# First offset convolution of each deformable layer in two row parts, column transposes between them, first batch of offsets loaded before the first column windows

## The chip, the cores and the metric

The kernel runs on one core of a Trainium2 chip. The time is the device time of one execution in microseconds; the number compared is the median over several executions. Engines of the core: PE (matmul, with PEld for its weight loads), DVE (vector), ACT (scalar), POOL (here only memsets and DMA issue), SP (DMA issue).

## What is computed

The input is 8 images of 16 channels, 64 x 64, float32. Four blocks follow each other: a gated scan over rows and columns; an inverted bottleneck (hidden convolution, depthwise 3 x 3, projection); two deformable convolutions; and two distance convolutions with batch norm. The change touches the two deformable convolutions. Each computes offsets by a plain 3 x 3 convolution, samples the image at the shifted places for the 9 taps, and contracts the samples with the weights:

```python
def deform_conv(x, w, b, ow, ob):
    off = conv2d(x, ow, ob).reshape(Bn, K, 2, Hh, Ww) * OFFSET_SCALE
    cy = iy[None, None, :, None] + dy[None, :, None, None] + off[:, :, 0]
    cx = ix[None, None, None, :] + dx[None, :, None, None] + off[:, :, 1]
    ...
    samp = gather(y0i, x0i, (1 - wy) * (1 - wx)) + gather(y0i, x0i + 1, (1 - wy) * wx) + ...
    out = jnp.einsum('bckhw,ock->bohw', samp, w.reshape(w.shape[0], Cin, K))
h = jax.nn.relu(group_norm1(deform_conv(x, w1, b1, ow1, ob1), g1, be1)) + x
h = jax.nn.relu(group_norm1(deform_conv(h, w2, b2, ow2, ob2), g2, be2)) + h
```

## The kernel before

The program of each engine is written out by hand, with semaphores between the engines; every engine runs its own list in the order written. Both deformable layers (L = 0 and 1) run the same code. The image lies in SBUF at `XA`, 128 partitions (8 images x 16 channels), rows padded. A layer has an opening stage and a sampling stage.

**Opening stage.** The offset convolution is cut into four blocks of 16 rows, m = 0 to 3. `convolve(m)` (L1301) uses the PE array as 16 tiles of 32 x 32: for each of the 9 taps, 4 groups of partitions i (two images each), 2 axes and 2 halves h of the block (8 rows of 64, so 512 columns), one matmul, in all 144. Results stand in four PSUM banks, 4 to 7 for even m and 0 to 3 for odd m (`conv_bank`). float32 matmuls show as two pairs of weight load and matmul in the trace, so 288 pairs a block. ACT copies the four banks with the bias into `RAW` (`copy_offsets`, L1075, by the line of its operation L1082); DVE bounds them and adds a ramp (`bound_offsets`, L714; L720 and L722) and takes the largest value (`reach`, L725, L727). SP stores the block to the DRAM tensor `offsets` in four transfers of 256 KB (`store_offsets`, L450, L455), then rearranges it there into `offsets_by_batch`, a batch being 4 rows of output with all taps (`arrange_batch`, L460; the issues carry L472; 10 transfers for batch 0 and 6 for each next one). Batch 0 needs rows 0 to 4 of the offsets. POOL loads a batch into SBUF, spread over partitions, four transfers of 576 or 624 KB (`load_batch`, L1520, L1528).

Between `convolve(0)` and `convolve(1)` PE transposes the image into columns (`turn_columns`, L1316, 64 matmuls that show as 128 pairs, L1320), ACT and DVE copy the results (L1072, L711), POOL stores them to the DRAM tensor `columns` (`store_columns`, L1493, L1501) and loads windows of them back by chunks (`load_windows`, L1506, L1515). DVE spreads the windows (L422).

The order of PE's opening stage:

```python
convolve(0)
...
    turn_columns(g_)
...
convolve(1)
...
convolve(2)
pe.wait_ge(s_cve, 16 * L + 8)
convolve(3)
pe.wait_ge(s_cve, 16 * (L + 1))
```

**Sampling stage.** 16 batches of 3 units. For each batch ACT computes distances (`distances`, L1085, L1089) as soon as it is loaded, DVE clips them (L739), and for each unit ACT makes two y terms (`y_terms`, L1091, L1098 and L1099), DVE three products (L745 to L747), PE the sample matmuls (L1341, L1346), ACT copies the samples (L1109), and every second batch PE contracts them (L1364). On ACT, `distances(L, 0)` and the y terms of units 0 and 1 stand behind `copy_offsets(L, 2)`, those of unit 2 behind `copy_offsets(L, 3)`. On DVE, `bound_offsets(L, 3)` stands behind batch 0. The first sample matmul waits for all copies of convolution 3.

## Time and profile before

| what | us |
|---|---|
| median of 3 runs | 822.86 (821.83 to 826.68) |
| the profiled execution's own time | 825.47 |
| its span, first to last instruction | 823.7 |
| opening stage, first layer (first matmul of convolution 0 to last of convolution 3) | 223.84 to 282.86 |
| opening stage, second layer | 476.12 to 531.35 |
| mean granted TensorE clock | 0.923 of full speed |

Times in a timeline are microseconds from the start of the span; a row of a timeline merges instructions of one line that follow closely, with their count (an x count is one of trace records, so of pairs for PE), and in brackets the idle time of the engine before it and what ended it. "Issue" there means that the profile shows nothing that the engine waited for. A few matmul records can be missing or fall into a neighbouring row, so counts can be off by some per cent. A stretch's row gives busy time and record count of each engine, the granted clock, the DMA share (mean busy share of the 16 DMA engines) and GB/s.

### The profile page before, as it was taken

Reading aid. Unit: us, or ns where it says so; the run is one execution under the profiler, and the core shown is the slowest. Engines: PE = TensorE matmul, PEld = TensorE weight load, DVE = VectorE, ACT = ScalarE, POOL = GpSimd, SP = SyncE. Lnnn points to the kernel's source line nnn. Section 1 sums busy time; section 2 is a strip of 40 time slices with the busy share of each in tenths; the row PEclk is TensorE's granted clock in tenths of the full one; section 3 lists DMA queues with packets and bytes.
Section 4 is the critical chain, followed back from the end, with each engine's and each line's share of the span. In section 5 each row is a group of like instructions: output and inputs, shape, how many; then the busy total and the mean of one; then the engine's idle time right before and its main releaser. Section 6 shows DMA issues by size and latency. Waiting matters only on the chain.

```text
span 823.7 us, 30308 instructions
## 1 busy us (share of the span) xinstructions
PE 638.3 (77%) x13948; PEld 426.9 (52%) x13948; DVE 588.9 (71%) x839; ACT 461.3 (56%) x624; POOL 136.3 (17%) x229
## 2 busy tenths in 40 slices
PE   3449999999997767888887588658878788749482
PEld 1224545467874346565555465347555555527251
DVE  6994350211342899999999744699999999984456
ACT  2725252532321668888888341557888889441513
POOL 1000000000023232333320004423333330000000
PEclk9869999999999779999999889869999999959596
DMA  4000000000037967777772006988777773000002
GB/s 170 0 0 3 3 2 3 2 18 4 12 91 230 371 206 257 257 244 250 247 237 101 2 11 190 347 277 266 243 244 251 258 242 127 3 1 4 1 3 103
DMA packets 28778, 108.73 MB, mean 132 GB/s; under 512 B 10612, under 2 KB 15412, under 8 KB 24552
## 3 DMA queue, kind: packets, MB, share of 16 engines
q0 software_dynamic: 14400, 86.80, 31.6%
q1 hardware_dynamic: 14248, 19.97, 7.8%
q8 instruction: 110, 1.80, 0.9%
q14 instruction: 20, 0.16, 0.1%
HBM read 91.84 MB, written 19.65 MB: 135 GB/s over the span
## 4 chain that ended last, share of the span: by engine, by line
PE 50%; DVE 37%; issue 6%; ACT 6%; DMA 1%; SPq 0%; DVEq 0%; ACTq 0%
PE psum L1261 14%; PE psum L1308 10%; DVE arena L746 7%; DVE arena L747 7%; DVE arena L745 6%; PE psum L1341 6%; PE psum L1237 5%; PE psum L1364 5%; PE psum L1453 4%; DVE arena L422 4%; DVE arena L739 3%; PE psum L1320 2%; PE psum L1460 2%; PE psum L1274 2%; DVE arena L622 1%
## 5 line engine op out<-in xcount | busy, mean ns | idle before, releaser
L1341 PE MATMUL psum<-arena 64*64 64x297 f32 (+4 forms) x4512 | 225.3, 348 | 77.4 <-DVE arena L747 72.4
L1341 PEld LDWEIGHTS psum<-arena 64*64 64x64 f32 x4512 | 162.9, 137 | 140.0 <-DVE arena L747 83.2
L1109 ACT ACTIVATE arena<-psum 128x792 f32<-128x792 f32 (+1 forms) x96 | 84.7, 883 | 65.1 <-PE psum L1341 58.4
L1528 POOL DMA_DIRECT2D arena<-offsets_by_batch x128 | 80.0, 639 | 224.2 <-DVE arena L747 163.7
L1261 PE MATMUL psum<-arena 32*32 32x512 f32 x3456 | 115.1, 597 | 0.3 <-DVE arena L669 0.3
L1308 PE MATMUL psum<-arena 32*32 32x512 f32 x2304 | 86.6, 646 | 19.3 <-issue 13.5
L745 DVE SCALAR_TENSOR_TENSOR arena<-arena 128x792 f32<-128x792 f32 (+3 forms) x96 | 92.6, 965 | 5.7 <-ACT arena L1099 4.3
L1261 PEld LDWEIGHTS psum<-arena 32*32 32x32 f32 x3456 | 73.6, 103 | 39.9 <-issue 13.8
L747 DVE SCALAR_TENSOR_TENSOR arena<-arena 128x792 f32<-128x792 f32 (+3 forms) x96 | 92.3, 961 | 0.0
L746 DVE SCALAR_TENSOR_TENSOR arena<-arena 128x792 f32<-128x792 f32 (+3 forms) x96 | 92.2, 961 | 0.0
L1099 ACT ACTIVATE arena<-arena 128x792 f32<-128x792 f32 (+3 forms) x96 | 88.2, 918 | 0.0
L1098 ACT ACTIVATE arena<-arena 128x792 f32<-128x792 f32 (+3 forms) x96 | 87.8, 915 | 0.0
L1045 ACT ACTIVATE arena<-psum,arena 128x512 f32<-128x512 f32 x48 | 29.8, 686 | 92.1 <-PE psum L1261 92.1
L1089 ACT ACTIVATE arena<-arena 128x2304 f32<-128x2304 f32 (+1 forms) x32 | 72.7, 2272 | 11.3 <-DMA arena<-offsets_by_batch 11.3
L1308 PEld LDWEIGHTS psum<-arena 32*32 32x32 f32 x2304 | 49.6, 106 | 52.4 <-issue 39.0
L659 DVE TENSOR_SCALAR arena<-arena 128x2048 f32<-128x2048 f32 x12 | 14.7, 1231 | 84.8 <-ACT arena L1045 84.8
L1364 PE MATMUL psum<-arena 64*64 64x256 f32 x1152 | 68.1, 381 | 2.3 <-ACT arena L1113 2.3
L1237 PE MATMUL psum<-arena 128*128 128x512 f32 x96 | 45.4, 621 | 21.7 <-DVE arena L630 21.7
L1501 POOL DMA_DIRECT2D columns<-arena x16 | 9.9, 760 | 302.7 <-DVE arena L711 237.3
L1082 ACT ACTIVATE arena<-psum,arena 128x512 f32<-128x512 f32 x32 | 19.7, 687 | 61.1 <-PE psum L1308 61.1
L1453 PE MATMUL psum<-arena 32*32 32x512 f32 x1152 | 44.1, 663 | 12.3 <-DVE arena L906 10.8
L1364 PEld LDWEIGHTS psum<-arena 64*64 64x64 f32 x1152 | 43.4, 131 | 18.2 <-ACT arena L1113 2.5
(148 smaller groups left out, 683.1 us busy)
## 6 DMA issues: line engine op xcount, KB each, us to landing
arena<-offsets_by_batch POOLq DMA_DIRECT2D x112, 576.0 KB, 7.9
arena<-offsets_by_batch POOLq DMA_DIRECT2D x16, 624.0 KB, 7.6
offsets<-arena SPq DMA_DIRECT2D x32, 256.0 KB, 9.0
offsets_by_batch<-offsets SPq DMA_DIRECT2D x184, 24.0 KB
arena<-columns POOLq DMA_DIRECT2D x24, 160.0 KB, 9.5
columns<-arena POOLq DMA_DIRECT2D x8, 320.0 KB, 6.7
arena<-in_x SPq DMA_DIRECT2D x4, 512.0 KB, 5.2
out<-arena SPq DMA_DIRECT2D x8, 256.0 KB, 2.2
```

What stands on the lines that cost most here:

```text
L745: v.scalar_tensor_tensor(term(0), term(0), 0.0, part(tx), ALU.min, ALU.mult)
L746: v.scalar_tensor_tensor(term(1), term(1), 1.0, part(tx), ALU.subtract, ALU.mult)
L747: v.scalar_tensor_tensor(term(2), part(ty), 0.0, part(tx), ALU.min, ALU.mult).then_inc(s_g, 1)
L1098: a.activation(term(0), part, ACT.Copy, scale=-1.0)
L1099: a.activation(term(1), part, ACT.Abs).then_inc(s_nd, 1)
L1109: ins = a.activation(ap(SAMP + n // 2 % 2 * SPAR + n % 2 * SLOTS * K * SX + u * WB[0], [[SR, 2], [SX, KR], [1, w]]), ap_ps(bank, [[CH, 2], ...
L1237: t_.matmul(ps(ch % 4, 0, CH), cols(W_HID + t * P, P), cols(XIN + ch * CH, CH), start=True, stop=True).then_inc(s_c1, 1)
L1261: ins = t_.matmul(ps_q(j, dw_bank(t, half) + i), cols(W_DIAG + (t * K + k) * Q, Q, Q * i, Q), ap(T_PAD[t % 4] + row * PW + k % 3, [[PW, CR ...
L1308: ins = t_.matmul(ps_q(2 * axis + h, conv_bank(m) + i), cols(W_CONV[L] + (axis * K + t) * Q, Q, Q * i, Q), ap(XA + (BLK * m + 8 * h + t // ...
L1341: ins = t_.matmul(ps_t(s, bank + r, first * K * w, many * K * w), window, ap(g_at(unit, d0) + first * TW + s * w, [[GS + TW, many], [SLOTS ...
L1364: ins = t_.matmul(ps_t(r, bank, (2 - k // 3) * SX, GR * SX), weights_, ap(SAMP + j % 2 * SPAR + r * SR + k * SX, [[K * SX, GR], [1, SX]], ...
L1528: g.dma_start(cols(in_at(n, 0), 2 * in_rows(n) * W, 64 * r + 32 * half, 32), bass.AP(batch_d.tensor, 2 * (4 * r * NB + n) * INS, [[0, QW / ...
```

## The change

Convolution 0 is cut by rows: of each 8-row half of the block first rows 0 to 4 (`FIRST = 5`, 320 columns a matmul, banks 4 to 7), and after the transposes rows 5 to 7 (192 columns, banks 0 to 3). The banks of convolutions 1, 2 and 3 swap accordingly. ACT's copies and DVE's bounding of block 0 are cut in the same way, the second pieces behind the column copies; `written` and `stored` give the new semaphore counts. SP stores rows 0 to 4 of the first half (two transfers) and rearranges batch 0 before it stores the rest of the block (four transfers). POOL issues the load of batch 0 ahead of the first window load and that of batch 1 ahead of the second. ACT no longer waits for the whole image before its first copies.

```diff
+FIRST = 5
...
-        def ps_q(quadrant, bank):
-
-            return psum[quadrant * Q:(quadrant + 1) * Q, bank, 0:CH]
+        def ps_q(quadrant, bank, off=0, n=CH):
+
+            return psum[quadrant * Q:(quadrant + 1) * Q, bank, off:off + n]
...
-        def conv_bank(m):
-
-            return 4 if m % 2 == 0 else 0
+        def conv_bank(m, first=0):
+
+
+            return 0 if m % 2 == 0 and m + first > 0 else 4
...
+        def written(L, m, end=CR):
+
+
+            return 20 * L + 4 * m + (8 if m or end == CR else 4)
+
+        def stored(L, m):
+
+
+            return (64 if m else 96) * (L + 1)
...
             def store_offsets(L, m):
-                sp.wait_ge(s_d1, 4 * L + m + 1)
+                sp.wait_ge(s_d1, 5 * L + m + 2)
+                for h in range(2):
+                    store_rows(m, h, FIRST if m == h == 0 else 0, CR)
+
+            def store_rows(m, h, first, end):
+
                 for axis in range(2):
-                    for h in range(2):
-                        sp.dma_start(bass.AP(off_d.tensor, axis * B * KP * N + (2 * m + h) * CH,
-                                             [[N, 2 * KP], [2 * KP * N, 4], [1, CH]]),
-                                     ap(D1 + m % 2 * NATS, [[CH, 4], [1, CH]], 64 * axis + Q * h, Q)
-                                     ).then_inc(s_ds[m], 16)
+                    sp.dma_start(bass.AP(off_d.tensor, axis * B * KP * N + (2 * m + h) * CH + first * W,
+                                         [[N, 2 * KP], [2 * KP * N, 4], [1, (end - first) * W]]),
+                                 ap(D1 + m % 2 * NATS + first * W, [[CH, 4], [1, (end - first) * W]],
+                                    64 * axis + Q * h, Q)).then_inc(s_ds[m], 16)
...
-                sp.wait_ge(s_ds[min(SLOTS * n + SLOTS, H - 1) // BLK], 64 * (L + 1))
+                m = min(SLOTS * n + SLOTS, H - 1) // BLK
+                sp.wait_ge(s_ds[m], stored(L, m) if n else 96 * L + 32)
...
             for L in range(2):
+                sp.wait_ge(s_d1, 5 * L + 1)
+                store_rows(0, 0, 0, FIRST)
+                arrange_batch(L, 0)
                 store_offsets(L, 0)
-                arrange_batch(L, 0)
                 arrange_batch(L, 1)
                 arrange_batch(L, 2)
...
-            def bound_offsets(L, m):
-
-                dve.wait_ge(s_cve, 16 * L + 4 * m + 4)
+            def bound_offsets(L, m, first=0, end=CR):
+
+                dve.wait_ge(s_cve, written(L, m, end))
                 if m >= 2:
-                    dve.wait_ge(s_ds[m - 2], 64 * (L + 1))
-                raw, d1 = RAW + m % 2 * NATS, D1 + m % 2 * NATS
-                link(v.tensor_scalar(cols(d1, NATS), cols(raw, NATS), con("minus_limit"), con("limit"), ALU.max,
-                                     ALU.min))
-                v.tensor_tensor(ap(d1, [[W, 4 * 8], [1, W]], 0, 64), ap(d1, [[W, 4 * 8], [1, W]], 0, 64),
-                                ap(CON + CONST["ramp"][0], [[0, 4 * 8], [1, W]], 0, 64), ALU.add).then_inc(s_d1, 1)
+                    dve.wait_ge(s_ds[m - 2], stored(L, m - 2))
+                rows = lambda at, pn: ap(at + m % 2 * NATS + first * W, [[CH, 4], [W, end - first], [1, W]], 0, pn)
+                link(v.tensor_scalar(rows(D1, P), rows(RAW, P), con("minus_limit"), con("limit"), ALU.max, ALU.min))
+                v.tensor_tensor(rows(D1, 64), rows(D1, 64),
+                                ap(CON + CONST["ramp"][0], [[0, 4], [0, end - first], [1, W]], 0, 64),
+                                ALU.add).then_inc(s_d1, 1)
...
             def layer2(L):
-                bound_offsets(L, 0)
+                bound_offsets(L, 0, 0, FIRST)
                 for g_ in (1, 3, 5, 7):
                     copy_columns(L, g_)
+                bound_offsets(L, 0, FIRST, CR)
                 reach(L, 0)
...
-            def copy_offsets(L, m):
+            def copy_offsets(L, m, first=0, end=CR):
                 if m >= 2:
                     act.wait_ge(s_red, 4 * L + m - 1)
-                    act.wait_ge(s_d1, 4 * L + m - 1)
+                    act.wait_ge(s_d1, 5 * L + m)
+                at, n = first * W, (end - first) * W
                 for i in range(4):
-                    act.wait_ge(s_cv, 16 * L + 4 * m + i + 1)
-                    a.activation(cols(RAW + m % 2 * NATS + i * CH, CH), ps(conv_bank(m) + i, 0, CH), ACT.Identity,
+                    act.wait_ge(s_cv, written(L, m, end) - 3 + i)
+                    a.activation(cols(RAW + m % 2 * NATS + i * CH + at, n), ps(conv_bank(m, first) + i, at, n), ACT.Identity,
                                  bias=cols(OB + L, 1)).then_inc(s_cve, 1)
...
             for L in range(2):
-                act.wait_ge(s_xa, NCH * (L + 1))
-                copy_offsets(L, 0)
+                copy_offsets(L, 0, 0, FIRST)
                 for g_ in (0, 2, 4, 6):
                     copy_columns(L, g_)
+                copy_offsets(L, 0, FIRST, CR)
                 copy_offsets(L, 1)
                 copy_offsets(L, 2)
                 distances(L, 0)
...
-                def convolve(m):
...
-                                    ins = t_.matmul(ps_q(2 * axis + h, conv_bank(m) + i),
+                                    ins = t_.matmul(ps_q(2 * axis + h, conv_bank(m, first) + i, first * W, (end - first) * W),
                                                     cols(W_CONV[L] + (axis * K + t) * Q, Q, Q * i, Q),
-                                                    ap(XA + (BLK * m + 8 * h + t // 3 + 1) * XW + t % 3 + 1,
-                                                       [[XW, CR], [1, W]], Q * i, Q),
+                                                    ap(XA + (BLK * m + 8 * h + first + t // 3 + 1) * XW + t % 3 + 1,
+                                                       [[XW, end - first], [1, W]], Q * i, Q),
...
                 pe.wait_ge(s_wc, 16 * (L + 1))
-                convolve(0)
+                convolve(0, 0, FIRST)
                 pe.wait_ge(s_xa, NCH * (L + 1))
                 for g_ in range(8):
                     if g_ == 4:
-                        pe.wait_ge(s_cve, 16 * L + 4)
+                        pe.wait_ge(s_cve, written(L, 0, FIRST))
                     turn_columns(g_)
                 pe.wait_ge(s_xta, 4 * L + 2)
                 pe.wait_ge(s_xtv, 4 * L + 2)
-                convolve(1)
+                convolve(0, FIRST, CR)
                 pe.wait_ge(s_xta, 4 * L + 4)
                 pe.wait_ge(s_xtv, 4 * L + 4)
+                convolve(1)
+                pe.wait_ge(s_cve, written(L, 0))
                 convolve(2)
-                pe.wait_ge(s_cve, 16 * L + 8)
+                pe.wait_ge(s_cve, written(L, 1))
                 convolve(3)
-                pe.wait_ge(s_cve, 16 * (L + 1))
+                pe.wait_ge(s_cve, written(L, 3))
                 pe.wait_ge(s_ws, 16)
...
             for L in range(2):
                 store_columns(L, 0)
                 store_columns(L, 1)
+                load_batch(L, 0)
                 load_windows(L, 0)
-                load_batch(L, 0)
+                load_batch(L, 1)
                 load_windows(L, 1)
-                load_batch(L, 1)
```

PE, from convolution 0 to the start of convolution 3 (one row may stand for many; `offsets_written` are ACT's copies of the banks). Before:

```order
L1308 MATMUL psum<-arena 32x512 [waits layer_result_in_padded_image,convolution_weights_loaded]
L1308 MATMUL psum<-arena 32x512 x143
L1320 MATMUL psum<-arena 64x128 [waits layer_result_in_padded_image]
L1320 MATMUL psum<-arena 64x128 x31
L1320 MATMUL psum<-arena 64x128 [waits offsets_written]
L1320 MATMUL psum<-arena 64x128 x31
L1308 MATMUL psum<-arena 32x512 [waits layer_result_in_padded_image,columns_copied_by_vector,columns_copied_by_scalar]
L1308 MATMUL psum<-arena 32x512 x143
L1308 MATMUL psum<-arena 32x512 [waits layer_result_in_padded_image,columns_copied_by_vector,columns_copied_by_scalar]
L1308 MATMUL psum<-arena 32x512 x143
L1308 MATMUL psum<-arena 32x512 [waits layer_result_in_padded_image,offsets_written]
```

And after the change:

```order
L1329 MATMUL psum<-arena 32x320 [waits layer_result_in_padded_image,convolution_weights_loaded]
L1329 MATMUL psum<-arena 32x320 x143
L1341 MATMUL psum<-arena 64x128 [waits layer_result_in_padded_image]
L1341 MATMUL psum<-arena 64x128 x31
L1341 MATMUL psum<-arena 64x128 [waits offsets_written]
L1341 MATMUL psum<-arena 64x128 x31
L1329 MATMUL psum<-arena 32x192 [waits layer_result_in_padded_image,columns_copied_by_vector,columns_copied_by_scalar]
L1329 MATMUL psum<-arena 32x192 x143
L1329 MATMUL psum<-arena 32x512 [waits layer_result_in_padded_image,columns_copied_by_vector,columns_copied_by_scalar]
L1329 MATMUL psum<-arena 32x512 x143
L1329 MATMUL psum<-arena 32x512 [waits layer_result_in_padded_image,offsets_written]
L1329 MATMUL psum<-arena 32x512 x143
```

One convolution of 144 matmuls has become two of 144, of 320 and of 192 columns, and the second stands behind the transposes, ahead of convolution 1.

SP's queue from the first store of a layer's offsets (`offsets_bounded` is DVE's bounding, `bounded_offsets_stored_0` the landing of block 0's store). Before:

```order
L455 DMA offsets<-arena 32x4x512 [waits offsets_bounded]
L455 DMA offsets<-arena 32x4x512 x3
L472 DMA offsets_by_batch<-offsets 8x3x256 [waits bounded_offsets_stored_0]
L472 DMA offsets_by_batch<-offsets 8x3x256 x3
L472 DMA offsets_by_batch<-offsets 8x3x192 x2
L472 DMA offsets_by_batch<-offsets 8x3x64 x4
L472 DMA offsets_by_batch<-offsets 8x3x256 [waits bounded_offsets_stored_0]
L472 DMA offsets_by_batch<-offsets 8x3x256 x5
```

And after the change:

```order
L471 DMA offsets<-arena 32x4x320 [waits offsets_bounded]
L471 DMA offsets<-arena 32x4x320
L489 DMA offsets_by_batch<-offsets 8x3x256 [waits bounded_offsets_stored_0]
L489 DMA offsets_by_batch<-offsets 8x3x256 x3
L489 DMA offsets_by_batch<-offsets 8x3x192 x2
L489 DMA offsets_by_batch<-offsets 8x3x64 x4
L471 DMA offsets<-arena 32x4x192 [waits offsets_bounded]
L471 DMA offsets<-arena 32x4x192
L471 DMA offsets<-arena 32x4x512 x2
L489 DMA offsets_by_batch<-offsets 8x3x256 [waits bounded_offsets_stored_0]
```

The store of block 0 has become two pieces, and the ten transfers of batch 0 stand between them; batches 1 and 2 and all later stores stand behind the second piece.

POOL's queue in the same stage. Before:

```order
L1515 DMA arena<-columns 64x5x144 [waits first_columns_stored]
L1515 DMA arena<-columns 64x144
L1515 DMA arena<-columns 64x5x144
L1515 DMA arena<-columns 64x144
L1528 DMA arena<-offsets_by_batch 32x1x4992 [waits offsets_arranged_0_of_four]
L1528 DMA arena<-offsets_by_batch 32x1x4992 x3
L1515 DMA arena<-columns 64x5x128 [waits first_columns_stored]
L1515 DMA arena<-columns 64x128
L1515 DMA arena<-columns 64x5x128
L1515 DMA arena<-columns 64x128
L1528 DMA arena<-offsets_by_batch 32x1x4608 [waits offsets_arranged_1_of_four]
```

And after the change:

```order
L1551 DMA arena<-offsets_by_batch 32x1x4992 [waits offsets_arranged_0_of_four]
L1551 DMA arena<-offsets_by_batch 32x1x4992 x3
L1538 DMA arena<-columns 64x5x144 [waits first_columns_stored]
L1538 DMA arena<-columns 64x144
L1538 DMA arena<-columns 64x5x144
L1538 DMA arena<-columns 64x144
L1551 DMA arena<-offsets_by_batch 32x1x4608 [waits offsets_arranged_1_of_four]
L1551 DMA arena<-offsets_by_batch 32x1x4608 x3
L1538 DMA arena<-columns 64x5x128 [waits first_columns_stored]
L1538 DMA arena<-columns 64x128
```

The load of batch 0 (4992 numbers a partition) has moved ahead of the first window load, that of batch 1 ahead of the second.

## Rows read from the trace of the kernel before

**Rows 1.** The page: busy time of each engine, and the chain that ended last.

```profile
PE 638.3 (77%) x13948; PEld 426.9 (52%) x13948; DVE 588.9 (71%) x839; ACT 461.3 (56%) x624; POOL 136.3 (17%) x229
...
PE 50%; DVE 37%; issue 6%; ACT 6%; DMA 1%; SPq 0%; DVEq 0%; ACTq 0%
```

**Rows 2.** Timeline of PE, first layer: start us, us, engine, line, instructions, idle before and its end.

```profile
233.59 7.21 PE L1320 MATMUL psum<-arena 128*64 128x128 f32 x128
240.73 10.48 PE L1308 MATMUL psum<-arena 32*32 32x512 f32 x298
254.09 10.21 PE L1308 MATMUL psum<-arena 32*32 32x512 f32 x256 [2.88 <-issue]
266.49 6.02 PE L1308 MATMUL psum<-arena 32*32 32x512 f32 x128 [2.19 <-issue]
273.33 4.51 PE L1308 MATMUL psum<-arena 32*32 32x512 f32 x128 [0.82 <-issue]
279.80 3.06 PE L1308 MATMUL psum<-arena 32*32 32x512 f32 x54 [1.96 <-issue]
284.52 0.96 PE L1341 MATMUL psum<-arena 64*64 64x198 f32 x8 [1.66 <-ACT arena L1082]
```

**Rows 3.** Timeline of PE, second layer, the same stage.

```profile
476.12 11.20 PE L1308 MATMUL psum<-arena 32*32 32x512 f32 x288 [5.82 <-DVE arena L946]
...
494.39 7.75 PE L1308 MATMUL psum<-arena 32*32 32x512 f32 x231
504.64 13.11 PE L1308 MATMUL psum<-arena 32*32 32x512 f32 x383 [2.50 <-issue]
518.12 4.51 PE L1308 MATMUL psum<-arena 32*32 32x512 f32 x128 [0.37 <-issue]
525.43 5.92 PE L1308 MATMUL psum<-arena 32*32 32x512 f32 x122 [2.80 <-issue]
```

**Rows 4.** The page: the DMA queue that carries instructions.

```profile
q8 instruction: 110, 1.80, 0.9%
```

**Rows 5.** DMA queue of instructions between 240.73 and 282.86 us: packets, MB, share.

```profile
q8 instruction: 6, 0.10, 0.9%
```

**Rows 6.** Stretches of both layers: us, busy of each engine, granted clock, DMA share, GB/s.

```profile
223.84:233.59 9.75, 9.75 (x301) 7.38 (x288) 2.73 (x4) 3.36 (x5) 0.00 (x0) 1.00 0.12 34
...
240.73:282.86 42.13, 34.28 (x866) 17.59 (x864) 22.20 (x23) 11.67 (x15) 17.99 (x28) 0.90 0.87 284
476.12:487.32 11.20, 11.20 (x290) 6.87 (x292) 2.63 (x4) 2.83 (x5) 0.00 (x0) 0.87 0.02 4
...
494.46:531.35 36.89, 31.22 (x864) 17.71 (x864) 18.62 (x18) 9.82 (x12) 18.24 (x28) 0.95 0.81 252
```

**Rows 7.** Timeline of DVE, second layer.

```profile
528.89 1.46 DVE L739 TENSOR_SCALAR arena<-arena 128x2496 f32<-128x2496 f32 x1 [2.58 <-ACT arena L1089]
...
536.55 0.97 DVE L745 SCALAR_TENSOR_TENSOR arena<-arena 128x780 f32<-128x780 f32 x1
...
540.42 1.35 DVE L720 TENSOR_SCALAR arena<-arena 128x2048 f32<-128x2048 f32 x1 [1.14 <-DMA offsets<-arena]
```

**Rows 8.** Timeline of ACT, second layer.

```profile
526.48 2.38 ACT L1089 ACTIVATE arena<-arena 128x2496 f32<-128x2496 f32 x1 [8.11 <-DMA arena<-offsets_by_batch]
...
534.46 0.89 ACT L1098 ACTIVATE arena<-arena 128x780 f32<-128x780 f32 x1
```

**Rows 9.** Timeline of SP's queue, first layer.

```profile
239.22 2.89 SPq L455 DMA_DIRECT2D offsets<-arena  x4
248.55 15.66 SPq L472 DMA_DIRECT2D offsets_by_batch<-offsets  x22
```

**Rows 10.** Timeline of POOL's queue, first layer.

```profile
241.04 5.04 POOL L1501 DMA_DIRECT2D columns<-arena  x8 [237.30 <-DVE arena L711]
...
258.07 2.18 POOL L1528 DMA_DIRECT2D arena<-offsets_by_batch  x4 [3.38 <-DMA offsets_by_batch<-offsets]
```

**Rows 11.** Timeline of PE, 254.09 to 254.3 us: matmuls that start in this fifth of a microsecond.

```profile
254.09 1.17 PE L1308 MATMUL psum<-arena 32*32 32x512 f32 x16 [2.88 <-issue]
```

3 lines of the change are left out of this document (2 added, 1 removed).

## The prediction

> **What bounds the kernel now.** I read the page first: PE is busy 77% of the span, and of the chain that ended last 50% is PE, 37% DVE and 6% "issue" [rows 1]. "Issue" is time in which the engine waits for nothing that the profile shows, so I looked for where it sits. The change touches one stage, which runs once per deformable layer, so the timeline of PE in that stage comes next [rows 2, 3]. The reader is to see two things there. The four offset convolutions and the column transposes run end to end, and the first sample matmul follows them at 284.52 us. And inside the convolutions PE stops for 2.88, 2.19, 0.82 and 1.96 us in the first layer and 2.50, 0.37 and 2.80 in the second, always with "issue" behind it. Between stops lie exactly 256, 128 and 128 matmul records (383 and 128 in the second layer). A matmul has a weight load of its own, so 128 pairs are 256 instructions.
>
> The queue that carries instructions explains this. It moved 110 packets with 1.80 MB in the whole run, 16.4 KB each [rows 4], and PE ran 2 x 13948 = 27896 instructions [rows 1], which is 254 to a packet. From 240.73 to 282.86 us it moved 6 packets [rows 5] for 864 pairs, 6.75 times 256 instructions. So PE's program arrives in blocks of 256, and where a stop ends after exactly 128 pairs PE has run out of program. From one restart to the next it is 273.33 - 266.49 = 6.84, 279.80 - 273.33 = 6.47 and 525.43 - 518.12 = 7.31 us: while the other queues fill the DMA engines a block takes about 6.9 us to come, however short its matmuls are. With the engines idle it takes at most what a block lasted in the first convolution without any stop, 9.75 / 2.25 = 4.33 us at a DMA share of 0.12 [rows 6].
>
> After the convolutions DVE is the bound (three tent products a unit), with no slack that gives a delay back; what the stage loses, the run loses.
>
> **What the first convolution costs in two parts.** The matmuls double: 144 of 512 columns become 144 of 320 and 144 of 192, and each is two pairs in the trace, so a layer gets 288 more pairs.
>
> (a) Streaming alone. A full-clock convolution is 9.75 us for 18 turns on each of the 16 tiles of the array, 542 ns a turn. The transposes give the cost of a column: 128 pairs in 7.14 us on two tiles are 112 ns for 128 columns [rows 2], at most 0.87 ns each. So 512 columns are 446 ns and some 96 ns are fixed. Turns of 320 columns then take 374 ns, of 192 columns 263 ns: 6.7 and 4.7 us, together 11.4, or +1.7 us. The bounds are +0 (all of the turn is columns) and +9.75 (none is).
>
> (b) Supply of instructions. At 6.7 us for 288 pairs a block would last 3.0 us, and at 4.7 us it would last 2.1. Both are below the 4.33 us of an idle system and far below 6.9. The short matmuls cannot run faster than their program comes. So I count blocks. The first part begins where the old one did; I take 8.0 us for it, between 6.7 (streaming) and 9.75 (supply). Transposes keep 7.14 us. The second part and the three whole convolutions are 288 + 864 pairs, 9 blocks. Before, the three took 42.13 us in the first layer and 36.89 in the second for 6.75 blocks [rows 6]: 6.24 and 5.47 us a block at DMA shares of 0.87 and 0.81.
>
> The bytes to be moved stay the same while the stretch grows, so the share falls. With a straight line from 4.33 us at no share to 6.9 at full share, and the new share as the old one times old length over new, about 0.71 and 0.66, the line gives 6.15 and 6.03 us. It also gives 6.57 and 6.41 for the old stretches, where 6.24 and 5.47 were measured, so I scale by 0.95 and 0.85: 5.84 and 5.14 us a block. First layer: 8.0 + 7.14 + 9 x 5.84 = 67.7 us against 59.02 (223.84 to 282.86), +8.7. Second layer: the granted clock is 0.87 over the first convolution (a part of it at 1.2 GHz, the rest at 2.4) after PE had idled, and it takes 11.20 us, 1.45 more [rows 6]. I keep that and take 9.4 for the first part: 9.4 + 7.14 + 46.3 = 62.8 us against 55.2 (476.12 to 531.35), +7.6. The sum is +16.3 us. At the unscaled measured rates it is 56.2 and 49.2 us for the nine blocks: +12.3 and +10.5, +22.8.
>
> The Trainium skill, "Runtime: NRT & Kernel Launch", section "Instruction fetch mechanics", says that a 16 KiB block of 256 instructions is fetched while the current one runs, and that crossing a block is mostly hidden. The blocks agree with the rows; "mostly hidden" does not, with 7.85 us of stops in one stage. By that rule the change would cost only (a), which is the first rival below.
>
> **What is gained.** Batch 0 no longer waits for the whole convolution 0. Before, its offsets went out at 239.22 us, the rearrangement started at 248.55 [rows 9], and the load was issued at 258.07 [rows 10]. After, the first part ends near 231.8; bank copies and bounding add some 4 us, and the store is two transfers of 160 KB in place of four of 256. I expect the rearrangement to start at about 240. Its ten transfers at 15.66 / 22 = 0.71 us each [rows 9] end at 247, so the load can go at about 249, nine microseconds sooner. What is it worth? In the first layer nothing: ACT's distances were done before DVE came to them. In the second DVE waited 2.58 us for them [rows 7], and ACT for the load until 526.48 [rows 8]. But the third unit of batch 0 needs ACT's y terms, which stand behind the copies of convolution 3, were started at 534.46 [rows 8] and took two operations of 0.89 us: they end at about 536.1, when DVE took the unit up at 536.55 [rows 7]. So of the 2.58 us some 0.4 is real; the end of convolution 3 is late next. The 1.14 us before DVE's bounding at 540.42 [rows 7] waits for an offset store and may go too. I count -1.5 us.
>
> **The other edits.** DVE: the bounding keeps its columns (1.35 us for the clamp of 2048 [rows 7]) in pieces of 1280 and 768, two instructions more, well under 0.5 us, while DVE is idle around both. ACT: four more copies, beside PE. POOL: the column stores (8 issues from 241.04 us, 5.04 us) start some 4 us sooner, since the transposes and the bounding ahead of DVE's column copies come sooner. Behind them the load of batch 0 now stands ahead of the first window load, and if its offsets were late the windows would be too; both are needed only when convolution 2 is copied, some 20 us on. SP: the store of the first block's rest waits for the second bounding, with the rearrangement of batches 1 and 2 and all later stores queued behind it. That bounding comes a whole convolution before the end of convolution 1, so batch 1, needed by ACT only after convolution 3, is in time. PE waits before convolution 1 for all column copies, and before 2 and 3 for the copies of convolutions 0 and 1, each done a convolution earlier. All of these cost nothing, except that the column stores and the load of batch 0 now fill the DMA engines while the 192-column part wants its blocks fastest; the block count holds that.
>
> **Sum.** 16.3 - 1.5 = +14.8 us. The profiled execution took 825.47 us, 2.6 over the median of 822.86; on it the sum gives 840.3, and against the median 837.7.
>
> **Rivals.**
> 1. Supply is not what binds the short matmuls, because a block is asked for early enough; then only (a) counts: +3.4 - 1.5 = about +2, 825 us. For it: the first convolution never stopped, with 4.33 us a block. In favour of it too: 16 matmuls start within 0.2 us after a restart [rows 11], so issuing is no limit. Against: three restarts in a row that came 6.5 to 7.3 us apart with PE empty between them.
> 2. The other side, faster: the crowd on the DMA engines moves forward. Column stores and the load of batch 0 (128 partitions of 4992 numbers, 2.5 MB, some 9 us at the 284 GB/s of [rows 6]) run during transposes, which need a block only every 7.14 us, and are gone before convolutions 2 and 3. Then the stops there go (2.19 + 0.82 + 1.96 and 0.37 + 2.80 = 8.1 us), with the 1.5 us above, against +3.4 of streaming and some 2 of new stops: -4, 819 us. It decides if the DMA share of the last two convolutions falls under about 0.5. Against: batches 1 and 2 are still loaded there.
> 3. Supply at the full price: every one of the nine blocks at about 6.9 us, 62.1 us, would give +18.2 and +23.5; with the measured rates it is +22.8 - 1.5 = +21, 844 us. I take 844 for this rival, as the share can't stay full in a longer stretch.
>
> **Chances.** Forecast and rival 3, one mechanism with two prices: 0.50 and 0.14. Rival 1: 0.27. Rival 2: 0.09. About 1%, 8.2 us, is what a measurement here can tell from no change. The forecast and rival 3 are slower by more than that but for a small part (0.04): slower 0.60. Rival 1 and half of rival 2 lie within 1%: same 0.35. Faster 0.05. The range for 8 in 10 goes from 823.5 (rival 1 with a little gained) to 848 (rival 3 and a bit more); the forecast's own range is 831 to 845.
>
> **What would show it.** In the changed profile: 288 more pairs a layer and 4.5 more packets on the instruction queue (110 to 114 or 115); the 192-column part lasting well over 4.7 us, with "issue" gaps inside it 128 pairs apart; restarts 5 to 7 us apart up to the first sample; the stage from the first matmul of convolution 0 to the last of convolution 3 lasting about 68 us in the first layer and 63 in the second; DVE without its 2.58 us wait in the second layer. I am wrong if the 192-column part takes 5 us, or if the gaps in convolutions 2 and 3 are gone.

## The result, and the profile after

The changed kernel takes 840.8 us (median of 4 runs, 839.3 to 841.9) where the kernel before took 824.3 in the same session: a ratio of 1.0196, 95% interval 1.0164 to 1.0229. It is slower, by 16.5 us; the prediction said 14.8. The profiled execution took 840.93 us with a span of 839.0, against 825.47 and 823.7.

The page of the changed kernel, first the busy time of the engines, then the instruction queue and the chain that ended last (before: [rows 1, 4]):

```profile
PE 645.2 (77%) x14524; PEld 438.3 (52%) x14524; DVE 589.8 (70%) x843; ACT 462.8 (55%) x632; POOL 135.7 (16%) x229
...
q8 instruction: 115, 1.88, 0.9%
...
DVE 42%; PE 41%; issue 7%; DMA 4%; ACT 4%; SPq 2%; DVEq 0%; ACTq 0%
```

There are 14524 - 13948 = 576 more pairs of weight load and matmul, 288 a layer, and five more packets of program. On the chain "issue" grew from 6 to 7%, and PE gave up first place to DVE, which says already that what ended late for DVE counts more than what ended late for PE.

The timeline of PE in the opening stage of the first layer (the counterpart of [rows 2]; columns as there):

```profile
224.90 5.08 PE L1329 MATMUL psum<-arena 32*32 32x320 f32 x191
230.33 2.36 PE L1329 MATMUL psum<-arena 32*32 32x320 f32 x85 [0.34 <-issue]
232.62 7.21 PE L1341 MATMUL psum<-arena 128*64 128x128 f32 x128
239.75 3.05 PE L1329 MATMUL psum<-arena 32*32 32x192 f32 x171
245.19 4.20 PE L1329 MATMUL psum<-arena 32*32 32x192 f32 x127 [2.39 <-issue]
251.49 10.25 PE L1329 MATMUL psum<-arena 32*32 32x512 f32 x256 [2.10 <-issue]
263.03 4.55 PE L1329 MATMUL psum<-arena 32*32 32x512 f32 x128 [1.29 <-issue]
269.06 4.51 PE L1329 MATMUL psum<-arena 32*32 32x512 f32 x128 [1.48 <-issue]
277.73 14.24 PE L1329 MATMUL psum<-arena 32*32 32x512 f32 x342 [4.16 <-issue]
296.05 0.59 PE L1362 MATMUL psum<-arena 64*64 64x198 f32 x8 [4.09 <-DVE arena L766]
```

The part of 320 columns lasts 8.0 us and already has a small stop. The part of 192 columns runs from 239.75 us to the end of its last matmul at 248.59 (the row from 245.19 also holds the first matmuls of convolution 1): 8.8 us for work whose streaming was put at 4.7, and it stops after 171 matmuls. All stops are in front of blocks: from the restart at 245.19 on, 127, 256, 128 and 128 records lie between them. They sum to 11.8 us, against 7.85 before. The last row shows something new: the first sample matmul waits 4.09 us for DVE's tent products, where before it waited for ACT's copies.

The same for the second layer (beside [rows 3]):

```profile
488.69 9.37 PE L1329 MATMUL psum<-arena 32*32 32x320 f32 x288 [5.82 <-DVE arena L966]
...
505.13 3.44 PE L1329 MATMUL psum<-arena 32*32 32x192 f32 x198
512.65 13.92 PE L1329 MATMUL psum<-arena 32*32 32x192 f32 x383 [4.08 <-issue]
527.61 17.34 PE L1329 MATMUL psum<-arena 32*32 32x512 f32 x512 [1.05 <-issue]
545.45 2.31 PE L1329 MATMUL psum<-arena 32*32 32x512 f32 x59 [0.49 <-issue]
```

Here the short part pays for one stop of 4.08 us (with it, it lasts 10.3 us). Three blocks (x383) and then four (x512) run without any stop: where [rows 3] has 0.37 and 2.80 us late in the stage, 1.05 and 0.49 are left.

The stretches (beside [rows 6]; start:end and length, then busy time and records of PE, PEld, DVE, ACT and POOL, the granted clock, the DMA share and GB/s):

```profile
224.63:232.62 7.99, 7.65 (x302) 5.57 (x289) 2.72 (x4) 3.34 (x6) 0.00 (x0) 1.00 0.15 41
239.75:291.97 52.22, 40.80 (x1154) 24.43 (x1152) 18.77 (x19) 13.09 (x19) 15.38 (x27) 0.87 0.84 259
...
505.13:547.76 42.63, 37.01 (x1154) 25.31 (x1152) 18.88 (x19) 12.39 (x18) 15.12 (x23) 0.92 0.67 198
```

From the first to the last matmul of the offset convolutions the first layer takes 67.3 us (224.63 to 291.97; 59.0 before), the second 59.1 (488.69 to 547.76; 55.2 before). That is 8.3 and 3.8 us, 12.1 in all, and less than the 16.5 lost. To find the rest I measured from one layer's start to the next. From the first convolution matmul of layer 1 to that of layer 2 it is 476.12 - 223.84 = 252.3 us before and 488.69 - 224.63 = 264.1 after: +11.8, for a stage only 8.3 longer. The timeline of DVE tells why. First layer, before:

```profile
269.47 1.35 DVE L720 TENSOR_SCALAR arena<-arena 128x2048 f32<-128x2048 f32 x1 [11.02 <-ACT arena L1082]
...
286.04 0.97 DVE L745 SCALAR_TENSOR_TENSOR arena<-arena 128x780 f32<-128x780 f32 x1 [1.41 <-ACT arena L1099]
```

First layer, after:

```profile
283.51 1.35 DVE L739 TENSOR_SCALAR arena<-arena 128x2048 f32<-128x2048 f32 x1 [11.64 <-ACT arena L1103]
...
298.60 0.97 DVE L764 SCALAR_TENSOR_TENSOR arena<-arena 128x780 f32<-128x780 f32 x1
```

From the bounding of block 2 (first row of each) DVE now runs without a hole into the products of the third unit (last row). The bounding starts when ACT has copied convolution 2. It came 14.0 us later, the third unit 12.56 us later (a wait of 1.41 us was there to absorb), and the second layer starts 12.57 us later. So it is the end of convolution 2, not of convolution 3, that now sets the end. Before, only the stops of 2.88 and 2.19 us lay ahead of it, 5.1 us; now all 11.8 us do (convolution 3 runs through). The second layer shows the same on DVE (beside [rows 7]):

```profile
539.20 1.35 DVE L739 TENSOR_SCALAR arena<-arena 128x2048 f32<-128x2048 f32 x1 [5.38 <-ACT arena L1103]
...
547.02 1.45 DVE L758 TENSOR_SCALAR arena<-arena 128x2496 f32<-128x2496 f32 x1
...
554.28 0.97 DVE L764 SCALAR_TENSOR_TENSOR arena<-arena 128x780 f32<-128x780 f32 x1
...
557.89 1.35 DVE L739 TENSOR_SCALAR arena<-arena 128x2048 f32<-128x2048 f32 x1 [0.88 <-DMA offsets<-arena]
```

The wait of 2.58 us for batch 0 is gone, as is every other wait up to the third unit; the wait for the store of offsets is 0.88 us instead of 1.14. From this layer's first matmul to its third unit it was 536.55 - 476.12 = 60.4 us and is 554.28 - 488.69 = 65.6, +5.2; what is left of it when DVE starts on the distance convolutions (734.94 us before, 752.35 after) is +4.8. The first layer started 0.8 us later in this execution, and the rest of the span was some 2 us shorter. That 2 us says nothing of the change: the same rest takes 86.7 to 89.4 us in the profiles of this study, whatever the kernel. Together 11.8 + 4.8 + 0.8 - 2.1 = 15.3, the difference of the spans.

SP's queue and POOL's in the first layer (beside [rows 9, 10]):

```profile
239.09 11.30 SPq L489 DMA_DIRECT2D offsets_by_batch<-offsets  x10
```

```profile
238.49 5.04 POOL L1524 DMA_DIRECT2D columns<-arena  x8 [234.75 <-ACT arena L1092]
251.88 2.19 POOL L1551 DMA_DIRECT2D arena<-offsets_by_batch  x4 [8.36 <-DMA offsets_by_batch<-offsets]
```

The rearrangement starts at 239.09 us, but its ten transfers take 1.13 us each, beside the column stores. The 0.71 us of the prediction was the mean of the 22 transfers of three batches; the ten of batch 0 alone took 0.78 each before (248.55 to 256.35 us). The load of batch 0 is issued at 251.88, 6 us sooner than before and not 9.

### The profile page after: what moved, and what is told of

Its sections match the earlier page's. It is cut to its first block, busy times and chain, and to the rows that moved or that the text cites. A ratio compares the mean times of both kernels' runs of the same rounds, so it can differ in the third digit from the quotient of the medians.

```text
span 839.0 us, 31477 instructions
## 1 busy us (share of the span) xinstructions
PE 645.2 (77%) x14524; PEld 438.3 (52%) x14524; DVE 589.8 (70%) x843; ACT 462.8 (55%) x632; POOL 135.7 (16%) x229
## 4 chain that ended last, share of the span: by engine, by line
DVE 42%; PE 41%; issue 7%; DMA 4%; ACT 4%; SPq 2%; DVEq 0%; ACTq 0%
PE psum L1282 14%; DVE arena L765 8%; DVE arena L766 7%; DVE arena L764 7%; PE psum L1329 6%; PE psum L1258 5%; DVE arena L434 4%; DVE arena L758 4%; PE psum L1476 4%; PE psum L1385 3%; PE psum L1362 3%; DMA offsets<-arena 3%; PE psum L1341 2%; PE psum L1295 1%; PE psum L1483 1%
## 5 line engine op out<-in xcount | busy, mean ns | idle before, releaser
L1362 PEld LDWEIGHTS psum<-arena 64*64 64x64 f32 x4512 | 163.2, 136 | 144.1 <-DVE arena L766 87.1
L1282 PE MATMUL psum<-arena 32*32 32x512 f32 x3456 | 115.0, 597 | 0.3 <-DVE arena L688 0.3
L1329 PE MATMUL psum<-arena 32*32 32x512 f32 (+2 forms) x2880 | 94.9, 575 | 23.2 <-issue 17.4
L1282 PEld LDWEIGHTS psum<-arena 32*32 32x32 f32 x3456 | 73.4, 103 | 39.9 <-issue 13.8
L1329 PEld LDWEIGHTS psum<-arena 32*32 32x32 f32 x2880 | 62.1, 109 | 53.5 <-issue 41.0
L1065 ACT ACTIVATE arena<-psum,arena 128x512 f32<-128x512 f32 x48 | 29.8, 687 | 92.1 <-PE psum L1282 92.1
L678 DVE TENSOR_SCALAR arena<-arena 128x2048 f32<-128x2048 f32 x12 | 14.7, 1233 | 84.7 <-ACT arena L1065 84.7
L1103 ACT ACTIVATE arena<-psum,arena 128x512 f32<-128x512 f32 (+2 forms) x40 | 21.4, 603 | 80.9 <-PE psum L1329 80.8
L739 DVE TENSOR_SCALAR arena<-arena 128x2048 f32<-128x2048 f32 (+2 forms) x10 | 11.3, 1135 | 71.1 <-ACT arena L1103 70.2
L1476 PE MATMUL psum<-arena 32*32 32x512 f32 x1152 | 44.7, 662 | 12.3 <-DVE arena L925 10.8
```

Of the source, the lines that this page charges most:

```text
L1282: ins = t_.matmul(ps_q(j, dw_bank(t, half) + i), cols(W_DIAG + (t * K + k) * Q, Q, Q * i, Q), ap(T_PAD[t % 4] + row * PW + k % 3, [[PW, CR ...
L1329: ins = t_.matmul(ps_q(2 * axis + h, conv_bank(m, first) + i, first * W, (end - first) * W), cols(W_CONV[L] + (axis * K + t) * Q, Q, Q * i ...
L1362: ins = t_.matmul(ps_t(s, bank + r, first * K * w, many * K * w), window, ap(g_at(unit, d0) + first * TW + s * w, [[GS + TW, many], [SLOTS ...
```

## The experiments

Two theories stand against each other. Supply: short matmuls cost what their program takes to arrive, so 288 more pairs a layer are 2.25 more blocks a layer at several us each. Streaming: they cost their fixed part only, +3.4 us in all by the prediction's sum. A third question came with the result: whether the new orders of SP and POOL, put at nothing, matter. Differences of a median are against the median of the kernel before in the same session, 824.9 us in all three; the changed kernel itself was measured once, against 824.3.

### The split alone

The kernel before, with only the 144 matmuls of convolution 0 made twice, for rows 0 to 4 and 5 to 7, one after the other ahead of the transposes:

```diff
 def convolve(m):
+    for first, end in (((0, 5), (5, CR)) if m == 0 else ((0, CR),)):
...
-        ins = t_.matmul(ps_q(2 * axis + h, conv_bank(m) + i),
+        ins = t_.matmul(ps_q(2 * axis + h, conv_bank(m) + i, first * W, (end - first) * W),
```

> The kernel before, with only PE's convolution 0 of each layer cut into 5 and 3 rows, both pieces back to back ahead of the transposes; no transfer, copy or order changed. Supply theory: 576 pairs are 4.5 blocks of program, at about 3.6 us a block with the DMA engines idle 16 us instead of 9.75, so +6.4 us a layer and +12 to +13 us in all (about 837). Streaming rival: 11.4 us instead of 9.75, +1.7 a layer, +3.4 in all (about 828). If the whole cost lay in the moved transfers, no more than +3.4 either.

Measured: 836.6 us, +11.7, ratio 1.0143 (1.0082 to 1.0204). PE in the first layer, convolution 0 in its two parts:

```profile
223.75 5.09 PE L1309 MATMUL psum<-arena 32*32 32x320 f32 x192
229.09 2.97 PE L1309 MATMUL psum<-arena 32*32 32x320 f32 x128 [0.25 <-issue]
232.56 2.32 PE L1309 MATMUL psum<-arena 32*32 32x192 f32 x128 [0.50 <-issue]
236.02 2.24 PE L1309 MATMUL psum<-arena 32*32 32x192 f32 x117 [1.14 <-issue]
```

Nothing but the split is new here, and the DMA engines have nearly nothing else to do (share 0.02 from 229.09 to 236.02 us). The restarts are 3.47 and 3.46 us apart (the same in the second layer: 491.67 to 495.14), though 128 pairs of 192 columns run in 2.3 us. So a block costs about 3.5 us even when nothing competes. The convolution takes 14.7 us in the first layer (223.49 to the first transpose at 238.18) instead of 9.75. The whole stages take 64.6 and 62.3 us, 5.6 and 7.0 more than before; the layers, counted as above, lose 5.7 and 4.4 us. In the first layer nearly the whole price is paid in the convolution itself.

Does streaming fall with this? The rows give an upper bound for it, with the drain before each stop counted in: 191 matmuls of 320 columns in 5.08 us and 128 of 192 in 2.32 are 7.7 and 5.2 us for 288, together 3.1 more than 9.75. That is more than the 1.7 of the prediction, but at most +6.2 us in all, against 11.7 measured.

The same split put where the DMA engines carry little else for a long time (share 0.02 from 128 to 180 us): four of the depthwise convolutions, of 288 pairs each, are cut into 5 and 3 rows (or 4 and 4) in the same way and so get 576. This was one execution.

```diff
+parts = {2: ((0, 5), (5, CR)), 3: ((0, 4), (4, CR))}.get(t, ((0, CR),))
+for first, end in parts:
...
-    ins = t_.matmul(ps_q(j, dw_bank(t, half) + i),
+    ins = t_.matmul(ps_q(j, dw_bank(t, half) + i, first * W, (end - first) * W),
```

> The disputed cost by itself, where nearly no transfer runs: the kernel before with four depthwise convolutions (tiles 2 and 3, two halves each) cut in two, tile 2 into 5 and 3 rows, tile 3 into 4 and 4; each goes from 288 to 576 pairs. Supply theory: the restarts are one block of 128 pairs and about 3.47 us apart (as in the split convolution 0 of the first experiment), so each takes 14.5 to 15.6 us instead of 9.7 and the kernel +19 to +23 us. Streaming rival: 11.4 us each, +7 us in all, and no issue gaps.

Measured: 849.3 us, +24.4, 6.1 us for each added 288 pairs, with 119 packets on the instruction queue (110 before). PE, two places:

```profile
132.15 2.32 PE L1263 MATMUL psum<-arena 32*32 32x192 f32 x128 [0.71 <-issue]
136.16 1.66 PE L1263 MATMUL psum<-arena 32*32 32x192 f32 x80 [1.69 <-issue]
...
165.42 2.75 PE L1263 MATMUL psum<-arena 32*32 32x256 f32 x128 [0.37 <-issue]
169.16 2.75 PE L1263 MATMUL psum<-arena 32*32 32x256 f32 x128 [0.99 <-issue]
```

The restarts are 4.01 us apart with 192 columns and 3.74 with 256. The matmuls differ by a fifth in length (2.32 against 2.75 us for 128) and the distance does not follow them; over these four convolutions it is 3.5 to 4.0 us.

The DMA records show the supply itself. A block is one packet of 16,384 bytes on the instruction queue. Its start, its duration and PE's restart behind it, in us (first layer):

| run | packet starts | takes | PE restarts | restart to next packet |
|---|---|---|---|---|
| split alone, engines idle | 230.24 | 1.03 | 232.56 | 1.05 |
| the same | 233.61 | 1.00 | 236.02 | 1.04 |
| kernel before, engines busy | 264.17 | 0.96 | 266.49 | 4.34 |
| the same | 270.83 | 0.95 | 273.33 | 4.02 |
| changed kernel, engines busy | 266.47 | 1.32 | 269.06 | 6.26 |
| the same | 275.32 | 0.97 | 277.73 | 3.76 |

In each row PE restarts 2.3 to 2.6 us after the packet's start, and the packet takes about 1 us, crowd or not. What the crowd stretches is the time from a restart to the start of the next packet: 1.0 us with idle engines, 3.8 to 6.3 with busy ones (share 1.01 from 264 to 282.86 us in the kernel before; 0.62, 0.90 and 1.02 in the changed one's stretches from 263, 269 and 275). So the stops are late blocks, and the blocks are late because their packets start late. What holds the packet back in the queue isn't shown.

### What the crowd does

The crowd was tested by taking it away. In both kernels the loads of batches 0 to 2 bring 64 numbers to each partition instead of 4608 or 4992. The rest of those batches' offsets isn't loaded, so their samples are made from what stood there; the number of instructions is the same.

```diff
-g.dma_start(cols(in_at(n, 0), 2 * in_rows(n) * W, 64 * r + 32 * half, 32),
+g.dma_start(cols(in_at(n, 0), 64 if n < 3 else 2 * in_rows(n) * W, 64 * r + 32 * half, 32),
```

> The kernel before with the loads of batches 0 to 2 of each layer cut to 64 numbers a partition instead of 4992 or 4608 (their samples are then computed from stale data). If the stops come from program blocks that wait behind other transfers: the stops after the load of batch 0 (2.19, 0.82 and 1.96 us; 2.80 in the second layer) go, the 2.88 and 2.50 beside the column stores stay, the opening stage takes 53 to 55 us instead of 59.0 and 51 to 53 instead of 55.2. If the stops have nothing to do with other transfers, they stay.

> The changed kernel with the same cut of the loads of batches 0 to 2. Supply theory: the stops beside the column stores stay, those in convolutions 1 to 3 go; the opening stage takes 56 to 60 us instead of 67.3 in the first layer, still 3 to 6 us more than the kernel before with the same cut. If the added pairs only cost streaming, 1.7 us more than that kernel.

Measured, one execution each: 817.9 us for the kernel before without these loads (-7.0), 827.2 us for the changed one without them (+2.3). PE in the first layer, of the kernel before without the loads:

```profile
241.24 10.40 PE L1308 MATMUL psum<-arena 32*32 32x512 f32 x298
254.81 20.36 PE L1308 MATMUL psum<-arena 32*32 32x512 f32 x566 [3.17 <-issue]
```

and of the changed kernel without them:

```profile
238.50 3.05 PE L1329 MATMUL psum<-arena 32*32 32x192 f32 x171
243.97 2.90 PE L1329 MATMUL psum<-arena 32*32 32x192 f32 x127 [2.41 <-issue]
250.28 29.44 PE L1329 MATMUL psum<-arena 32*32 32x512 f32 x854 [3.41 <-issue]
```

Behind the column stores no stop is left in the first layer: 566 and 854 matmuls run through. The three later stops of [rows 2] (2.19, 0.82 and 1.96 us) and the three of 1.29, 1.48 and 4.16 us above thus go with the batch loads; the first ones, which stay, lie beside the column and offset stores. In the second layer one stop of 1.32 us is left before the change, and stops of 3.16 and 0.56 us after it. Between these two kernels the change costs 9.3 us, more than the 6.2 that streaming can cost at most. Measured inside the two layers, where it acts, it is 5.3 and 6.0 us, against 11.8 and 4.8 with the loads. So the loads' share in the full price is some 5 to 7 us (16.6 - 11.3, or 16.5 - 9.3), from single executions.

### The orders of SP and POOL, taken one by one

The changed kernel with SP's order undone (block 0 stored whole, then batch 0 rearranged, the awaited counts with it):

```diff
-                sp.wait_ge(s_d1, 5 * L + 1)
-                store_rows(0, 0, 0, FIRST)
-                arrange_batch(L, 0)
                 store_offsets(L, 0)
+                arrange_batch(L, 0)
```

> The changed kernel with SP's part undone: block 0 is stored whole in four transfers after its second bounding, and batch 0 is rearranged after that. Supply theory: the pairs stay, so the time stays within 2 us of the changed kernel (839 to 843); batch 0 comes later again, which may cost up to 3 us. Rival that the early store and rearrangement crowd the DMA engines in the 192-column part: 3 to 8 us faster than the changed kernel (833 to 838).

The changed kernel with POOL's order undone:

```diff
+                load_windows(L, 0)
                 load_batch(L, 0)
-                load_windows(L, 0)
-                load_batch(L, 1)
                 load_windows(L, 1)
+                load_batch(L, 1)
```

> The changed kernel with POOL's part undone: windows ahead of each of the first two batch loads. Supply theory: within 1.5 us of the changed kernel. Rival that POOL's order costs time: 3 us or more faster than the changed kernel.

Measured: SP's order undone 835.2 us, ratio 1.0137 (1.0088 to 1.0186); POOL's undone 841.5 us, 1.0226 (1.0164 to 1.0288). POOL's order shows no price, though its four runs lie far apart (836.9 to 845.7). SP's seems to cost some 5 us of the 16.5. The stretches of six microseconds in the changed kernel:

```profile
257.00:263.00 6.00, 4.74 (x145) 3.14 (x125) 0.00 (x0) 0.69 (x1) 0.00 (x0) 1.00 0.98 357
263.00:269.00 6.00, 4.55 (x128) 2.50 (x127) 2.96 (x2) 1.85 (x3) 2.05 (x4) 1.00 0.62 142
```

and in the one with SP's old order:

```profile
257.00:263.00 6.00, 6.00 (x205) 4.94 (x199) 0.00 (x0) 1.51 (x3) 0.00 (x0) 1.00 0.12 30
263.00:269.00 6.00, 6.00 (x207) 5.10 (x181) 5.02 (x3) 0.91 (x2) 4.34 (x8) 1.00 0.33 97
```

With batch 0 rearranged and loaded later, the DMA engines stand almost empty (0.12 and 0.33) in a stretch in which PE runs convolutions 1 and 2, and it gets 205 and 207 pairs into six microseconds instead of 145 and 128. Its convolutions then run 639 matmuls without a stop.

A weaker form: the changed kernel with its early store kept, and batch 0 rearranged only when all of block 0 has landed.

```diff
-                arrange_batch(L, 0)
                 store_offsets(L, 0)
+                arrange_batch(L, 0)
```

> The changed kernel, but SP rearranges batch 0 only after the whole of block 0 is stored and has landed; the early store of rows 0 to 4 stays. If the ten transfers of the rearrangement and the early load of batch 0, beside the 192-column part and convolutions 1 and 2, are what costs 5.6 us more than with SP's old order, 834 to 836. If it is the cutting of the store into smaller pieces, 839 to 842.

Measured: 835.6 us, ratio 1.0126 (1.0074 to 1.0178), with 639 and 767 matmuls in a row without a stop in the two layers. So it is the early rearrangement and what follows it, not the store in two pieces. The interval just overlaps that of the changed kernel (1.0164 to 1.0229), as the other did; two kernels that agree make the 5 us likely, not certain. Where they are lost is less sure still: the profiled execution of the kernel with only POOL's order undone keeps SP's new order, and its first layer took 257.4 us, like those without it (255.6 and 257.7), not 264.1.

Now the other way round, the orders put into the kernel before, without the split. Both; then each alone:

```diff
-                store_offsets(L, 0)
+                store_offsets(L, 0, (0,))
                 arrange_batch(L, 0)
+                store_offsets(L, 0, (1,))
```

The halves (0,) and (1,) are rows 0 to 7 and 8 to 15 of the block; batch 0 needs rows 0 to 4 and waits for the first half only. POOL's order is that of the change.

> The kernel before with the orders alone: convolution 0 whole; SP stores the first half of block 0 (two transfers), rearranges batch 0, then stores the second half; POOL loads batches 0 and 1 ahead of the windows. No pair is added. Supply theory: the time of before or up to 2 us less (822 to 825), with DVE's wait for batch 0 in the second layer gone and the end of convolution 3 late next. Rival that the orders cost what the change lost: +3 us or more.

> The kernel before with POOL's new order alone (batches 0 and 1 loaded ahead of the windows). If the gain of orders alone (5.3 us) is POOL's, about 819 to 821. If it is SP's, or needs both, within 1.5 us of before (823 to 826).

> The kernel before with SP's new order alone (half of block 0 stored, batch 0 rearranged, other half stored). If the gain of orders alone is SP's, 819 to 821. If it needs POOL's order too, 823 to 826.

Measured, 10 runs each: both orders 819.6 us, ratio 0.9936 (0.9909 to 0.9963); POOL's alone 823.1, 0.9994 (0.9973 to 1.0016); SP's alone 817.1, 0.9917 (0.9889 to 0.9946). This is the surprise of the study: the order that costs on the split kernel gains 7.8 us on the kernel before. PE in the first layer, with SP's order alone:

```profile
240.44 9.95 PE L1310 MATMUL psum<-arena 32*32 32x512 f32 x298
251.52 13.10 PE L1310 MATMUL psum<-arena 32*32 32x512 f32 x384 [1.13 <-issue]
266.92 8.11 PE L1310 MATMUL psum<-arena 32*32 32x512 f32 x182 [2.31 <-issue]
```

Against [rows 2] the stops are 1.13 and 2.31 us in place of 2.88, 2.19, 0.82 and 1.96, and the stage lasts 51.5 us (223.53 to 275.03) instead of 59.0. In the second layer it is 54.1 instead of 55.2. The two sum to 8.6 us for the 7.8 measured. Of the first layer's 7.5 us, 4.4 are stops and 3.1 are PE's busy time in the stage (48.1 us instead of 51.2, at a granted clock of 0.97 instead of 0.93; a row's busy time counts the drain ahead of each stop too). The profiles with both orders (51.5 us) and with POOL's alone (60.5 us) put the first layer's gain on SP too.

### Holding the loads back

If the loads of batches 1 and 2 make the later stops, letting POOL issue them only when convolutions 2 and 3 are computed should remove these. It was tried on the kernel with both orders and on the changed kernel:

```diff
                 pool.wait_ge(s_ar[n % 4], arranged(L, n))
+                if n in (1, 2):
+                    pool.wait_ge(s_cv, 16 * L + (12 if n == 1 else 16))
```

(with 20 * L + 16 and + 20 in the changed kernel, whose count differs)

> Orders alone (the fourth experiment), and POOL holds the load of batch 1 until convolution 2 is computed and that of batch 2 until convolution 3 is. If the loads' crowd causes the stops in convolutions 2 and 3 (1.11 and 2.33 us, 2.26 in the second layer), they go: 1 to 4 us less than orders alone (816 to 819). If batch 1 or 2 then comes too late for ACT, it is slower than orders alone by up to 4 us.

> The changed kernel with the loads of batches 1 and 2 held until convolutions 2 and 3 are computed. If the crowd of these loads on the DMA engines makes the stops in convolutions 2 and 3 (1.29, 1.48 and 4.16 us in the first layer), 834 to 838. If only the pairs and the transfers of the rearrangement count, 839 to 843.

Measured: 817.9 us, ratio 0.9930 (0.9901 to 0.9959), against 0.9936 without the hold; and 837.2 us, 1.0174 (1.0121 to 1.0226), against 1.0196. Neither can be told from its kernel without the hold.

On the kernel with both orders the hold never came to bear, and this run says nothing of the loads. POOL's issue of the load of batch 1, without the hold and with it:

```profile
269.68 3.56 POOL L1530 DMA_DIRECT2D arena<-offsets_by_batch  x4 [9.30 <-DMA offsets_by_batch<-offsets]
```

```profile
270.30 4.72 POOL L1532 DMA_DIRECT2D arena<-offsets_by_batch  x4 [9.24 <-DMA offsets_by_batch<-offsets]
```

Both wait for the rearrangement, which lands later than convolution 2 ends. So this load is issued behind both stops of the first layer (they end at 252.24 and 267.68 us without the hold, at 253.05 and 268.75 with it), and these stops, 1.11 and 2.33 us, then 1.29 and 2.59, can't be its work. Ahead of the second one the load of batch 0 (issued at 255.65 us without the hold), windows and the rearrangement of batches 1 and 2 were on the queues; which of them made the block late isn't separated.

On the changed kernel the hold did act. POOL and PE in the first layer:

```profile
274.60 2.93 POOL L1553 DMA_DIRECT2D arena<-offsets_by_batch  x4 [19.16 <-PE psum L1329]
```

```profile
267.40 13.05 PE L1329 MATMUL psum<-arena 32*32 32x512 f32 x383 [1.20 <-issue]
282.82 4.92 PE L1329 MATMUL psum<-arena 32*32 32x512 f32 x87 [2.37 <-issue]
```

The load of batch 1 goes out at 274.60 us instead of 266.95. The stop of 4.16 us, which came one block behind the restart at 269.06, is gone: behind the restart at 267.40 three blocks run through, and only then, behind the held load, comes a stop of 2.37. The hold moved the stop and made it smaller. The run's time can't be told from the changed kernel's, so holding is no cure.

## Why the prediction was right

The sum came within 2 us, for a reason that held and with several terms that were sized wrong and cancelled. That it came so close is luck.

- **Supply, not streaming.** Right. The split alone costs 11.7 us where streaming gives 3.4 by the prediction and 6.2 at most by the rows; 6.1 us for each 288 pairs in another place; blocks of 128 pairs come 3.5 to 4.0 us apart with idle DMA engines; and each restart follows the packet of its block. Rival 1 falls. The Trainium skill, "Runtime: NRT & Kernel Launch", section "Instruction fetch mechanics", says that crossing a block is mostly hidden. The traces don't bear this out: with idle DMA engines it is hidden only where 128 pairs last longer than 3.5 us or so, and with full ones even the 4.5 us of 128 full-length pairs are too short.
- **The lengths.** The first part was taken at 8.0 and 9.4 us and lasted 8.0 and 9.37. The nine blocks were taken at 5.84 and 5.14 us and measured 52.22 / 9 = 5.80 and 42.63 / 9 = 4.74. The stages were to last 67.7 and 62.8 us and lasted 67.3 and 59.1. The share of the DMA engines was put at 0.71 and 0.66 and was 0.84 and 0.67, so the first layer's hit was two errors against each other: at 0.84 the scaled line gives 6.2 us a block, not 5.80. The second layer's share was right and its price of 5.14 too high. There rival 2 came true in part: after the 4.08 us stop of the short part three blocks and then four ran without a stop, and the expected +7.6 became +3.8. From 527.61 us on the share was 0.55, close to the 0.5 that rival 2 asked for. Gaps that go from convolutions 2 and 3 were named as what would make the forecast wrong; in this layer they shrank to 1.05 and 0.49 us.
- **"What the stage loses, the run loses."** This step failed in its place. It took the end of convolution 3 as what is late next. In the changed kernel DVE runs without a hole from the bounding of block 2, so the end of convolution 2 sets the time. In the first layer 6.7 us of new stops lie ahead of that end, and it lost 11.8 us with a stage 8.3 longer; the second lost 4.8 with a stage 3.8 longer. The slack that the prediction ruled out was in [rows 7] and in the DVE row at 286.04 above: waits of 2.58 and 1.41 us that a later bounding first had to fill.
- **Batch 0 ahead, -1.5 us.** Of the waits it named the 2.58 us one went and the 1.14 us one shrank to 0.88, but this paid nothing by itself: counted from its layer's first matmul, DVE came to batch 0 in the second layer 5.6 us later than before (547.02 - 488.69 against 528.89 - 476.12), so the gain of an earlier load was covered by the bounding's delay.
- **"All of these cost nothing."** Not contradicted for POOL's order (0.9994 alone on the kernel before) and false of SP's. Two experiments put its cost at about 5 us on the split kernel, and it is worth -7.8 us on the kernel before. The prediction let the crowding be held by the block count; but how much of a block's price is crowd depends on which transfer stands where. Without SP's order the same split measured +10.3 us, 4.5 below the forecast: the hit owes some 5 us to a term put at nothing. The ten transfers at 0.71 us each were 1.13 each, beside the column stores.

Put as a table of medians against the kernel before:

| | old order of SP | new order of SP |
|---|---|---|
| convolution 0 whole | 0 | -7.8 (-5.3 with POOL's) |
| convolution 0 in two parts | +10.3 (+11.7 in place, POOL's old) | +16.5 |

The lower left is the changed kernel with SP's old order, 835.2 us. The new order is not quite the same edit in both rows: below, rows 0 to 4 are stored before the second part is even computed, above, rows 0 to 7 after the whole convolution. The two edits are no sum: the new order gains without the split and costs with it. What the runs show of this is where it costs: the load of batch 0 fills the stretch (0.98 and 0.62 against 0.12 and 0.33) in which the split kernel has blocks to fetch. Why it gains without the split is shown only as stops that became fewer. One stretch of the kernel before,

```profile
254.00:260.00 6.00, 5.91 (x143) 3.18 (x151) 4.45 (x2) 0.00 (x0) 2.62 (x6) 0.73 0.32 91
```

and the same stretch with SP's order alone,

```profile
254.00:260.00 6.00, 6.00 (x191) 3.15 (x163) 3.71 (x2) 0.00 (x0) 4.73 (x8) 1.00 0.94 244
```

speak against a simple rule: the DMA share there rises from 0.32 to 0.94, and PE does more. A share alone doesn't say which block is late. That needs each transfer's place against each block's request, and it stays open.

The version to keep is the kernel before with SP's order alone: 817.1 us, ratio 0.9917, faster than both.

## What to carry to other kernels

Count a split in instructions before counting it in columns: when 128 pairs of weight load and matmul run in less than the 3.5 us that their program takes to arrive (6.0 to 8.7 us with the DMA engines full), shorter matmuls are not faster, and each piece costs the full price of its instructions. Look for the signature first, stops with "issue" behind them that lie a whole number of blocks apart, then for the packet of the instruction queue that starts some 2.4 us ahead of each restart. And test a change of queue order apart from the change it serves: here the order was the part worth having, and the split beside it cost more than the order gains. Before a hold is read as a test, the trace must show that it held something.
